# New order of turns and sums in the second attention, and the last fp4 products moved from GpSimd to VectorE

## What is computed

```python
# the second attention (random features), H = 16 heads of 8, m = 32
xw  = einsum('bhtd,hmd->bhtm', x, proj); xw = xw - max(xw, -1)
phi = exp(xw) * exp(-0.5 * sum(x * x, -1)) + eps       # of Q and of K
KV, Ksum = einsum('bhtm,bhtd->bhmd', phiK, V), sum(phiK, axis=2)
out = einsum('bhtm,bhmd->bhtd', phiQ, KV) / (einsum('bhtm,bhm->bht', phiQ, Ksum) + eps)

# fp4 (E2M1) along the last dim in blocks of 16, for x, h and the weights
scale = max(|xb|) / 6;  xn = xb / scale;  q = GRID[searchsorted(MID, |xn|)] * sign(xn) * scale
h = silu(x @ w_gate) * (x @ w_up);  out = q(h) @ q(w_down)      # hidden size 352
```

## Time and profile before

| what | us |
|---|---|
| median of 3 runs | 1044.42 |
| lowest and highest | 1042.56, 1044.64 |
| the profiled execution's own time | 1036.55 |
| its span in the trace | 1034.8 |
| TensorE busy | 906.0 (88%) |
| VectorE busy | 787.1 (76%) |

### The profile page before, as it was taken

How to read it: one execution, slowest core, us unless ns; L and a number is a source line. 1 busy time by engine, 2 the same in 40 slices (tenths; PEclk the granted TensorE clock), 3 DMA queues, 4 the chain that set the end, 5 groups by cost and what they waited for, 6 DMA issues and landing times.

```text
span 1034.8 us, 16383 instructions
## 1 busy us (share of the span) xinstructions
PE 906.0 (88%) x5966; PEld 514.3 (50%) x5988; DVE 787.1 (76%) x1853; ACT 414.9 (40%) x686; POOL 369.4 (36%) x460
## 2 busy tenths in 40 slices
PE   8899999999999898879989875799999878988786
PEld 3344444444433465554434342565667456766454
DVE  5578888767788677788767679747666998788985
ACT  2445565554433354333534356123222334331233
POOL 6282333223343453422444320323021344343433
PEclk9899999999999988889999987899999899998889
DMA  5363122202000000000000000000000000000000
GB/s 130 97 177 103 48 69 62 73 1 108 0 1 1 1 2 1 1 1 2 0 1 1 1 0 2 2 1 1 1 2 1 1 1 1 2 1 3 1 10 31
DMA packets 11531, 24.32 MB, mean 24 GB/s; under 512 B 1323, under 2 KB 7635, under 8 KB 11315
## 3 DMA queue, kind: packets, MB, share of 16 engines
q1 hardware_dynamic: 11152, 22.30, 7.4%
q10 hardware_dynamic: 294, 0.91, 0.3%
HBM read 15.69 MB, written 7.34 MB: 22 GB/s over the span
## 4 chain that ended last, share of the span: by engine, by line
PE 57%; DVE 32%; issue 4%; POOL 3%; ACT 2%; DMA 0%; DVEq 0%; POOLq 0%; ACTq 0%
PE ps L1082 4%; PE ps L1075 4%; PE ps L1069 4%; PE ps L419 4%; PE ps L369 3%; DVE a_MN L549 2%; PE ps L2166 2%; DVE XN L166 2%; PE ps L389 2%; PE ps L2163 2%; DVE g_C L1922 2%; PE ps L2769 2%; DVE r_PP L2818 2%; PE ps L2177 1%; PE ps L1051 1%
## 5 line engine op out<-in xcount | busy, mean ns | idle before, releaser
L1322 POOL TENSOR_TENSOR f_Y<-f_Y,f_TT 128x512 f32<-128x512 f32 x54 | 69.9, 1294 | 126.9 <-DVE f_TT L1168 126.8
L549 DVE TENSOR_REDUCE a_MN<-ps 128x1 f32<-128x384 f32 (+3 forms) x154 | 93.1, 637 | 25.1 <-PE ps L372 23.4
L119 POOL TENSOR_TENSOR rs<-t,mhalf 128x4 f32<-128x4 f32 x36 | 37.4, 1038 | 131.5 <-DVE t L102 130.3
L673 ACT ACTIVATE a_PT<-ps 128x1024 f32<-128x1024 f32 x56 | 57.4, 1025 | 58.3 <-PE ps L389 58.1
L1082 PE MATMUL ps<-f_HH,pack_zero 128*128 128x512 f32 x128 | 67.7, 611 | 10.1 <-DVE f_TT L1168 10.1
L1268 ACT ACTIVATE f_HH<-ps,pack_zero 128x512 f32<-128x512 f32 x64 | 44.0, 687 | 71.1 <-PE ps L1069 71.1
L1069 PE MATMUL ps<-f_XS,pack_zero 128*128 128x512 f32 x128 | 67.6, 610 | 1.4 <-DVE f_XS L1037 0.9
L1075 PE MATMUL ps<-f_XS,pack_zero 128*128 128x512 f32 x128 | 68.7, 619 | 0.0
L1168 DVE SCALAR_TENSOR_TENSOR f_TT<-ps,pack_zero,f_X 128x512 f32<-128x512 f32 x64 | 47.7, 745 | 27.5 <-PE ps L1082 26.7
L369 PE MATMUL ps<-a_KS,a_QS 72*128 72x128 bf16 (+3 forms) x224 | 53.8, 303 | 8.2 <-DVE a_MN L549 7.2
L769 POOL TENSOR_SCALAR_AFFINE_SELECT a_PT<-a_PT 128x256 f32<-128x256 f32 x64 | 26.2, 413 | 87.8 <-ACT a_PT L673 87.2
(11 more groups left out here) (342 smaller groups left out, 2191.8 us busy)
## 6 DMA issues: line engine op xcount, KB each, us to landing
scratch<-a_parts SPq DMA_DIRECT2D x16, 384.0 KB, 3.3
a_QS<-scratch SPq DMA_DIRECT2D x14, 288.0 KB
a_KS<-scratch SPq DMA_DIRECT2D x42, 96.0 KB
pack_one<-in_one SPq DMA_DIRECT2D x1, 2694.5 KB, 9.5
pack_zero<-in_zero SPq DMA_DIRECT2D x3, 884.5 KB, 4.6
X<-in_x SPq DMA_DIRECT2D x4, 256.0 KB, 10.3
out_x<-X SPq DMA_DIRECT2D x4, 256.0 KB, 2.0
a_QS<-a_MT SPq DMA_DIRECT2D x42, 4.0 KB
```

Of the source, the lines that this page charges most:

```text
L549: dve.tensor_reduce(M.a_MN[:, n % 2, ti, h0:h0 + k], bank(M, M.bank["a_max", n, jj], 128 * (ti + 1) * k).rearrange("p (a c) -> p a c", a=k ...
L673: act.activation(M.a_PT[:, c % 8, 0:1024], M.ps[:, a * 512:a * 512 + 1024], ACT.Exp).then_inc(made.sem, made.tick(n, hh))
L1322: pool.tensor_tensor(M.f_Y[:, i, :], M.f_Y[:, i, :], M.f_TT[:, u % 3, :], ALU.add).then_inc(made.sem, made.tick(n, u))
```

## The change

In the second attention:

- VectorE masks the sums of batch b - 1 before the first `subtract` of batch b, not after its second.
- TensorE computes the key features of groups 2 and 3 ahead of `queries(b - 1, 0)` and `(b - 1, 1)`, not behind them.
- The fillers (4, 6, 2 in batches 1, 2, 3) ahead of `queries(b - 1, 0)` and the 4 ahead of `queries(b - 1, 2)` go. There are now 3 and 2 inside these calls, behind the wait for the bank, and 2 ahead of the query features of groups 2 and 3.

In the second fp4 network's last passes:

- The product with the rate of pass 7 is VectorE's, directly behind the rate, and the power of two of pass 7 follows that of pass 6, ahead of the rounding of pass 5.
- The second products of passes 5, 6 and 7 are VectorE's, each directly behind its rounding. `down(5..7)` wait for VectorE.
- The fillers ahead of `down(6)` and `down(7)` (3 and 2) go, and ScalarE makes the step of pass 7 ahead of its copies of `down(5)`.

```diff
@@ attn_b_tensor @@
-        if b == 0 and w == "k" and pair[0] == 0:
-            filler(pe, M, 2, 2)
+        if (b, w, pair[0]) == (0, "k", 0) or (b and w == "q" and pair[0] == 2):
+            filler(pe, M, 2 + pair[0], 2)
...
-    def queries(b, j):
+    def queries(b, j, fill=0):
         made = S["p_qturn"]
         bk = spare("p_q", b, j)
+        filler(pe, M, bk, fill)
         if j == 0:
             pe.wait_ge(S["p_exp"].sem, S["p_exp"].at(8 * b + 7))
...
             features_output(pe, S, M, b - 2, spare())
-        if b:
-            filler(pe, M, 4, (0, 4, 6, 2)[b])
-            queries(b - 1, 0)
-            queries(b - 1, 1)
         features(b, "k", (2, 3))
         if b:
+            queries(b - 1, 0, 3)
+            queries(b - 1, 1)
             sums_turned(b - 1)
-            if b >= 2:
-                filler(pe, M, 2, 4)
-            queries(b - 1, 2)
+            queries(b - 1, 2, 2)
             queries(b - 1, 3)
@@ attn_b_vector @@
     for b in range(4):
+        if b:
+            sums(b - 1)
         for w in "kq":
             for g in range(4):
                 subtract(b, w, g)
-                if w == "k" and g == 1 and b:
-                    sums(b - 1)
@@ the second fp4 network @@
-FILL = {5: (8, 5, 2, 5, 2, 0, 0, 0), 7: (8, 4, 2, 2, 2, 2, 3, 2)}
+FILL = {5: (8, 5, 2, 5, 2, 0, 0, 0), 7: (8, 4, 2, 2, 2, 2, 0, 0)}
+
+def last_passes(n, u):
+    return n == 7 and u >= 5
...
         filler(pe, M, 4, FILL[n][u])
-        pe.wait_ge(S["q_hq"].sem, S["q_hq"].at(n, u))
+        done = S["q_round"] if last_passes(n, u) else S["q_hq"]
+        pe.wait_ge(done.sem, done.at(n, u))
@@ quant_up_vector @@
     rate(dve, S, M.q_A[:, i, :], M.q_R[:, i, :], S["q_rate"], n, u)
+    if (n, u) == (7, 7):
+        v = S["vec"]
+        dve.wait_ge(S["q_rate"].sem, S["q_rate"].n)
+        dve.tensor_tensor(blocks(M.q_V[:, i, :]), flat(M.q_HH, i), wide16(M.q_R[:, i, :]), ALU.mult).then_inc(v.sem, v.tick())
     if u:
         quant_bits(dve, S, M, n, u - 1)
+    if (n, u) == (7, 7):
+        dve.wait_ge(v.sem, v.n)
+        powers(dve, M.q_V[:, i, :], M.q_E[:, i, :], S["q_power"], n, u)
@@ quant_ffn_vector @@
         dve.wait_ge(S["q_step"].sem, S["q_step"].at(n, u))
-        rounded(dve, S, M.q_V[:, u % 4, :], M.q_E[:, u % 4, :], S["q_round"], n, u)
+        if not last_passes(n, u):
+            rounded(dve, S, M.q_V[:, u % 4, :], M.q_E[:, u % 4, :], S["q_round"], n, u)
+            return
+        v, made = S["vec"], S["q_round"]
+        rounded(dve, S, M.q_V[:, u % 4, :], M.q_E[:, u % 4, :], v)
+        dve.wait_ge(S["q_turned"].sem, S["q_turned"].at(n, 2 * (u - 4) + 1))
+        dve.wait_ge(v.sem, v.n)
+        dve.tensor_tensor(flat(M.q_HQ, u % 4), blocks(M.q_V[:, u % 4, :]), wide16(M.q_A[:, u % 4, :]), ALU.mult).then_inc(made.sem, made.tick(n, u))
...
-            quant_bits(dve, S, M, n, 7)
+                quant_bits(dve, S, M, n, 7)
@@ quant_ffn_scalar @@
+        if (n, u) == (7, 8):
+            exact(7)
         if u >= 3:
             down(u - 3)
...
-        if 1 <= u <= 8:
+        if 1 <= u < 8 or (n, u) == (5, 8):
             exact(u - 1)
@@ quant_ffn_gpsimd @@
-        if 2 <= u <= 8:
+        if 2 <= u <= 8 and not last_passes(n, u - 2):
             scale(u - 2)
-        if u == 8:
+        if u == 8 and n == 5:
             scale(7)
-        if u < 8 and (n == 5 or u):
+        if u < 8 and (n == 5 or 0 < u < 7):
             quant_scaled(pool, S, M, n, u)
```

## The result

| | before | changed |
|---|---|---|
| median, us | 1043.49 | 1031.43 |
| lowest and highest | 1039.87, 1044.64 | 1028.39, 1033.81 |
| runs | 4 | 4 |
| profiled execution | 1036.55 | 1033.81 |

Ratio 0.9889, 95% interval 0.9852 to 0.9926: 7.7 to 15.4 us faster. The forecast was 5.8 us. 1033.28 lies inside the range. So the 12 of the first comparison held some luck of the runs, and 5.8 was too little by either.

A forecast was written before the change was run, and what follows sets the result against it. It saw VectorE and TensorE waiting on each other in the second attention, and a VectorE, GpSimd, TensorE chain in the last passes. Gains 4.6 + 1.2 = 5.8 us from 1044.42 gave 1038.6 us, range 1032 to 1043.5.

The forecast's parts named there:

- the ring: Second attention: VectorE awaits features behind TensorE's turned queries, which await a bank VectorE frees late; VectorE waits 1.84, 4.06, 3.14 us.
- Group 2 of batch 2: Second attention, batch 2: VectorE's key group 2 starts at 402.9 and not at 407.00, 4.1 us earlier.
- Batch 1: Second attention, batch 1: TensorE loses a wait of 1.05 us, added fillers cost 0.6, gain 0.4 us.
- The full-clock price of the tail: Last passes: with TensorE at full clock the last multiplication starts at 1026.2 and ends at 1028.9, gain 2.6 us.
- the charge for half clock in the attention: Second attention: half clock behind TensorE's waits lowers the gain of batch 2 from 3.8 to 2.4 us, of batch 3 to 1.8.
- its three terms: Second attention at full clock: gains of 0.4 us in batch 1, 3.8 in batch 2 and 2.4 in batch 3.
- the pessimistic end: Second attention, batch 2: half clock until 409.7 stretches 4.5 us of work by 2.2 us, leaving a gain of 1.6.
- the upper end: Second attention, batch 3: group 2 starts near 432.4, not 434.80, the 2.4 us that top the range 0.5 to 2.4.
- slower: Rival, chance 0.09: in the attention, TensorE with fewer fillers gets added half clock in batches 2 and 3, 2.2 us lost, 1046.6.
- The clock stays up: Rival, chance 0.12: TensorE at full clock behind the new waits in attention and last passes, 9.2 us gained, 1035.2.
- The half clock eats most: Rival, chance 0.14: half clock in batches 2, 3 and the last passes leaves about 1.5 us, 1042.9, no change that can be told.
- the reorder would not reach TensorE: Rival on the attention: TensorE's issued order does not change or the bank is still held; counted in the no-change case, 0.14.

The follow-up runs named there:

- e5: Kernel before with VectorE's attention edit alone, the sums masked ahead of the first key group; ratio 0.9953, 4.9 us under before.
- e6: Kernel before with TensorE's attention edits alone (features ahead of turns, new fillers), mask behind the second key group; ratio 0.9920, 8.3 us under before.
- e4: Changed kernel without its seven new fillers per batch in the attention; ratio 0.9939, 6.4 us under before.
- e8: Changed kernel without new fillers in batch 1 and with 16 fillers ahead of the turns of pass 5; ratio 0.9909 to before.
- e11: Changed kernel with the 3 and 2 fillers ahead of the last two turns kept; ratio 0.9942 to before, last passes 16.03 us.
- e9: Changed kernel with the three second products on GpSimd again and the fillers 3 and 2 back; ratio 0.9965 to before, last passes 17.78 us.
- e1: Kernel before with the new attention code of TensorE and VectorE, last passes as before; ratio 0.9951, 5.1 us under before.

## Why the prediction was wrong

**The steps that held.** VectorE's three waits ahead of key group 2 did go (one of 1.45 us is left in batch 3, where the features came at half clock), by the ring as told; e5 and e6 show that either edit takes them away in batches 1 and 2. Group 2 of batch 2 was to start at 402.9 against a first difference at 400.7; it started at 403.25 with that at 401.04, the forecast to 0.1. Batch 1: 0.9 for 0.4; its seven fillers cost 0.4 to 0.6 us (20.54 to 20.68 against 20.10 in e4 and e8), where 0.2 each made 1.4. In the last passes the terms came out in three traces of four: products of 0.89 us for 0.9, pass 5 turned 0.8 us later, TensorE the bound through the first multiplication, 1.5 us for 1.2. That is partly luck: e4 had 0.4, by a longer half clock. The full-clock price of the tail, 2.6 us, is borne out by e8 (16.06 - 13.68 = 2.4). One reason was wrong: the 3 + 2 fillers were to cost nothing that counts, and e11 shows that without their removal the gain of the tail is nil. The estimate of 0.79 us for a product, from the Trainium skill, "VectorE: DVE Perf Modes", section "The perf-mode tier table", was 0.1 too low. It scaled the time of 2048 elements down in proportion, and a part of an instruction's time does not shrink with it: 128x16 elements take 0.17 us here (L1525). The row of the nearest instruction (0.88) had it right.

**The step that failed: the charge for half clock in the attention.** At full clock its three terms were 0.4 + 3.8 + 2.4 = 6.6 us; I took off 1.4 in batch 2 and 0.6 in batch 3 and wrote 4.6. It measured 6.9 (100.38 - 93.44), so the charge was not there. For batch 2 I wrote 3.8 us at full clock, 1.6 at half clock, and took 2.4, "because the row that is nearest (2.79 us idle, then 0.50) is one of half clock". It measured 4.2. From the last difference of one batch to that of the next, where the mask's new place does not shift the start, batch 2 is 28.23 against 24.23: 4.0 us, the 3.8 of full clock and a little.

The wait itself was foreseen: where the clock is full, TensorE does stand 2.2 us for the addition to X (e8). The half clock behind it was not there. In five of the seven traces with the new order and its fillers it began earlier, between 398 and 401 us, and stretched features, fillers and turns that were done before the addition to X (in the changed kernel TensorE was at the turned sums at 405.14); in e8 and e9 there was none in batch 2. I had moved the half clock of the old kernel along to the new wait, "at the same moment as before". I had also counted the new fillers as time only. e4 hints at what they hold: without them batch 2 is 2.3 us longer, and half clock lies where the pessimistic end had it. In batch 3 it was the same: half clock from 422 to 432 lay on the output, the features and the turns, VectorE was left a wait of 1.45 us, and the stage gained 2.3 us, the upper end (2.4), where I had taken 1.8.

**The sum.** 4.6 + 1.2 = 5.8 stood for 6.94 + 1.53 = 8.5. Of the 12.1 us of the first comparison the other 3 to 4 are the runs: with more of them it is 9.2, and the stages explain that within its interval. I had widened the range for such differences, but around a sum that was too small. (In the rival "slower" the quotient is 18.5 and not 18.6; nothing turns on it.)

**The rivals.** "The clock stays up" (9.2 us, 0.12) had the size of the attention right (6.6 for 6.9) and not the mechanism: in the changed kernel the clock did not stay up in batch 2, it was low where nothing waited for it. That the total too is the measured 9.2 is luck: its tail of 2.6 came only in e8. "The half clock eats most" and "slower" did not come; the extra stretch of half clock that the latter wanted in batch 2 shows only in e4, and there once. TensorE of the changed kernel did find its clock lowered anew in batches 2, 3 and the tail, as "the half clock eats most" has it, but it cost next to nothing in batches 2 and 3, and 0.8 us in the tail (14.53 against 13.68 in e8). That the reorder would not reach TensorE is refuted by the rows of the changed kernel and by e5 and e6.

## What to carry to other kernels

A half clock costs only what it stretches on the path: ask at what time its work must be done, not whether it falls, and credit a reorder with the half clock that it takes off the path of the old kernel. Two edits that each open the same ring of waits don't add up, but may each be needed in another batch, so price them per batch. Fillers are part of a hand-over: once a wait is gone, the fillers that filled it cost their own time (e11). When executions of one kernel spread by 1%, compare stages between two named instructions, in more than one trace: here many repeat to 0.02 us where whole runs move by 14, but the same last passes took 14.5 us three times and 15.7 once.

## What the runs showed that I had not expected

The same attention takes its half clock at different places from trace to trace without batch 2 noticing: in batch 2 it is from 398.2 to 405.0 in the changed kernel, from 399.4 to 402.8 in e1, and not at all in e8 and e9, and batch 2 is 24.50, 24.48, 24.47 and 24.49 us. How long TensorE had stood does not settle it alone: it fell to 0.50 during a wait of 1.01 us in the changed kernel, and stayed at 1.00 through one of 2.22 us in e8. Granted clock, single microseconds, the changed kernel:

```profile
398.00:399.00 1.00, 0.73 (x3) 0.76 (x4) 0.90 (x3) 0.00 (x0) 0.00 (x0) 0.61 0.00 0
404.00:405.00 1.00, 1.00 (x7) 1.00 (x5) 0.90 (x3) 0.34 (x2) 0.92 (x2) 0.50 0.00 0
```

and e8, in the middle of its wait and behind it:

```profile
404.00:405.00 1.00, 0.00 (x0) 0.00 (x0) 0.86 (x3) 1.00 (x2) 0.92 (x2) 1.00 0.00 0
...
406.00:407.00 1.00, 0.82 (x6) 0.63 (x7) 0.96 (x5) 0.53 (x2) 1.00 (x1) 1.00 0.00 0
```

Which moments of TensorE's idleness decide stays open; no run here was made to tell. What it does to the 550.7 to 556.8 us of untouched stages was not traced further either.
